# Attention scores by 64-row matmuls without the zero half of the keys, even and odd heads in two PSUM banks

## The chip, the cores and the metric

The kernel runs on one core of one Trainium2 chip. The metric is the device time of one launch in microseconds (us). A core has several engines that run side by side and meet at semaphores: TensorE (PE: matmuls, PEld: its weight loads), VectorE (DVE), ScalarE (ACT), GpSimd (POOL) and SyncE (SP, which starts DMA transfers). Matmuls write to PSUM, which is cut into eight banks; all else lives in SBUF, 128 partitions wide.

## The reference

One layer of a graph network: 128 graphs of 64 nodes, 512 channels, 8 heads of 64 channels.

```python
nx = _layernorm(x, ln1_g, ln1_b)
q = (nx @ Wq + bq).reshape(B, S, HEADS, HEAD_DIM)      # B = 128 graphs, S = 64 nodes
k = (nx @ Wk + bk).reshape(B, S, HEADS, HEAD_DIM)
v = (nx @ Wv + bv).reshape(B, S, HEADS, HEAD_DIM)
scores = jnp.einsum('bqhd,bkhd->bhqk', q, k) / np.sqrt(HEAD_DIM)
scores = jnp.where(adj_mask[:, None, :, :], scores, NEG)
attn = jax.nn.softmax(scores, axis=-1)
out = jnp.einsum('bhqk,bkhd->bqhd', attn, v).reshape(B, S, H)
x = x + (out @ Wo + bo)
nx = _layernorm(x, ln2_g, ln2_b)
return x + jax.nn.gelu(nx @ W1 + b1, approximate=False) @ W2 + b2
```

All is float32. Attention stays inside a graph: for each graph and head a 64 x 64 matrix of scores, over 64 channels.

## The kernel before

The 8192 nodes are cut into 16 groups (`NG`) of 512 nodes; a group has 4 tiles (`TILES`) of 128 nodes, and a tile holds two graphs. Phase one does layernorm, attention and its projection, group by group, and stores x1 to DRAM. Phase two loads x1 again and does the MLP, group by group.

Each large product is taken as three matmuls in the fast float32 form (`split3`, L154 to L156), from operands split into a high and a low part. The small products of the attention (scores, transposes of the probabilities, probabilities times v) are plain float32 matmuls.

Every engine has its own instruction stream, written out by hand, with semaphores between them. On TensorE the list `ORDER` sets the order inside a group's body:

- "U" n: one of 12 units of 12 matmuls that make q, k (transposed: channels on partitions) and v of the next group, into one of four PSUM banks `lin`.
- "S" t: `score`, the scores of tile t of this group.
- "P" t: `prob_transposes`; "O" t: `attend`, probabilities times v; "W" t: `project`.

So "S" 0 is followed by two units, "S" 1 by a unit, "P" 0 and a unit, "S" 2 directly by "O" 0, and "S" 3 by "W" 0. The last group has the order `LAST_ORDER`, in which fewer matmuls lie between the scores.

The scores before. The 128 partitions of `qT` and `kT` hold 64 channels of an even head (rows 0 to 63) and 64 of the odd head behind it (rows 64 to 127); m counts the four pairs of heads. A matmul that runs over all 128 rows would add the two heads. So `kT` is stored with a zero half: for each pair, tile and graph it has 128 columns, 64 in which only the rows of the even head are filled, 64 in which only those of the odd head are. POOL writes the zeros once for each of the two buffers (`zero_kT`, L461), ACT fills one half of the rows at a time (`take_k`, L538, two activations of 64 x 512 for each unit). `score` (L1042) then needs one matmul for each pair m and graph a: 128 rows of qT by 64 columns held in the array, 128 columns streamed. The output of graph a lands on partitions 64a to 64a+63, so the two graphs use the two column halves of the array.

`ps_scores` has two banks, one for the even tiles and one for the odd ones. The matmuls of a tile wait until DVE has read the scores of two tiles before (`wait(pe, masked, n - 1)`). DVE reads them in `mask_and_shift` (L762): it copies the scores where the adjacency is set into a buffer that POOL has filled with a large negative number.

At the start POOL's stream is: small constants, zeros for kT buffer 0, the first rstd, half of wq_lo and all of wk_lo (the low parts of the weights, L465), zeros for kT buffer 1, zeros for `probT` (L474), the second rstd. DVE's stream at that time splits the first normalised inputs into `nxT_hi` (L746) and `nxT_lo` (L748), four of each, one for each 128 channels; the first unit on TensorE waits for each of the four (`nx_split`).

Of the kernel before, what the change touches and what calls it, by code (L numbers as in the profile page):

```python
# [38 lines left out]
P = 128  # L39
# [119 lines left out]
def adj_layer(nc, x_dram, adj, ln1_g, ln1_b, ln2_g, ln2_b, wq, bq, wk, bk, wv, bv, wo, bo, w1, b1, w2, b2, out_dram):  # L159
# [7 lines left out]
    with ctx:  # L167
# [23 lines left out]
        with ExitStack() as phase:  # L191
            sb = placer(phase)
            wqkv_hi, wqkv_lo = ([sb(f"w{c}_{s}", [P, KC, HID], F32R) for c in "qkv"] for s in ("hi", "lo"))
            nxT_hi = sb("nxT_hi", [P, KC, GT], F32R)
            nxT_lo = sb("nxT_lo", [P, KC, GT], F32R)
            z1T = sb("z1T", [P, KC, GT])
            x = [sb(f"x{i}", [P, TILES, HID]) for i in range(2)]


            qT0 = sb("qT0", [P, KC, GT])  # L200
            kT0 = sb("kT0", [P, TILES, KC, 2, 2, NODES])
            v0 = sb("v0", [P, TILES, HID])
            early_end = nc.sbuf_base

            wo_hi, wo_lo = (sb(f"wo_{s}", [P, KC, HID], F32R) for s in ("hi", "lo"))
            xres = sb("xres", [P, 2, HID])
            bv_all = sb("bv_all", [P, HID])
            bo_all = sb("bo_all", [P, HID])
            qT = [qT0, sb("qT1", [P, KC, GT])]
            kT = [kT0, sb("kT1", [P, TILES, KC, 2, 2, NODES])]  # L210
            v = [v0, sb("v1", [P, TILES, HID])]
            softmax = sb("softmax", [P, 2, 2, HEADS, NODES])
            scores, expd = softmax[:, 0], softmax[:, 1]
            prob = sb("prob", [P, 2, HEADS, NODES])


            probT = sb("probT", [P, 2, KC, 2, 2, NODES])
            attT_hi = sb("attT_hi", [P, 2, HID], F32R)
            attT_lo = sb("attT_lo", [P, 2, HID], F32R)
            mask = sb("mask", [P, 2, TILES, NODES], U8)  # L220
            w_hi, w_lo = wqkv_hi + [wo_hi], wqkv_lo + [wo_lo]
# [21 lines left out]

        with ExitStack() as phase:
            lin = [phase.enter_context(nc.psum_tensor(f"lin{i}", [P, GT], F32)) for i in range(LIN)]
            ps_scores = phase.enter_context(nc.psum_tensor("ps_scores", [P, 2, HEADS, NODES], F32))
            ps_probT = phase.enter_context(nc.psum_tensor("ps_probT", [P, 2, KC, P], F32))
        with ExitStack() as phase:
            ps_out = [phase.enter_context(nc.psum_tensor(f"ps_out{i}", [P, HID], F32)) for i in range(TILES)]
# [13 lines left out]
        w_loaded, w_hi_done, w_lo_done = ([sem(f"w{c}_{s}") for c in "qkvo"] for s in ("loaded", "hi_done", "lo_done"))  # L263
        cols_loaded, rows_loaded, mlp_cols_loaded = sem("cols_loaded"), sem("rows_loaded"), sem("mlp_cols_loaded")
        filled, ident_done = sem("filled"), sem("ident_done")
        k_zeroed, probT_zeroed = sem("k_zeroed"), sem("probT_zeroed")
        stats_done, moments_done, var_done = sem("stats_done"), sem("moments_done"), sem("var_done")
        rstd_done, zn_done, t_done = sem("rstd_done"), sem("zn_done"), sem("t_done")
        z_transposed = sem("z_transposed")
# [3 lines left out]
        shifted, exp_done, sum_done, inv_done = sem("shifted"), sem("exp_done"), sem("sum_done"), sem("inv_done")  # L273
        prob_done, pt_done, probT_done = sem("prob_done"), sem("pt_done"), sem("probT_done")
        o_done, att_hi_done, att_split = sem("o_done"), sem("att_hi_done"), sem("att_split")
        mask_passed, fill_passed, stats_passed = sem("mask_passed"), sem("fill_passed"), sem("stats_passed")
        proj_done, xres_biased, x1_done = sem("proj_done"), sem("xres_biased"), sem("x1_done")

# [124 lines left out]
        def _(pool):  # L403
# [53 lines left out]
                for t in range(TILES):  # L457
                    bias_x1(g, par, t)

            def zero_kT(par):  # L460
                pool.memset(kT[par][:, :, :, :, :, :], 0.0).then_inc(k_zeroed, 1)  # L461

            def weight_lo(i, part):
                pool.wait_ge(w_hi_done[i], 1)
                pool.tensor_tensor(w_lo[i][:, part, :], raw_w[i][:, part], w_hi[i][:, part, :].bitcast(F32),  # L465
                                   ALU.subtract).then_inc(w_lo_done[i], 1)

            zero_kT(0)
            rstd_of(0)
            weight_lo(0, slice(KC // 2, KC))  # L470
            weight_lo(1, slice(0, KC))
            zero_kT(1)
            for par in range(2):
                pool.memset(probT[:, par], 0.0).then_inc(probT_zeroed, 1)  # L474
            rstd_of(1)
# [25 lines left out]
        def _(act):  # L501
# [31 lines left out]

            def take_k(g, par, m, bank):
                act.wait_ge(u_done, units_through(g, 3 * m + 1))
                for h in range(2):
                    rows = slice(h * HD, (h + 1) * HD)
                    act.activation(kT[par][rows, :, m, :, h, :],  # L538
                                   lin[bank][rows, :].rearrange("p (t a n) -> p t a n", a=2, n=NODES), ACT.Identity,
                                   bias=cols[rows, 3, m:m + 1]).then_inc(k_done, 1)  # L540

            def exponent(g, t):
                act.wait_ge(shifted, TILES * g + t + 1)
# [126 lines left out]
            for m in range(KC):  # L670
                take_q(0, 0, m, bank_of(-1, "U", 3 * m))
            weight_hi(3)
            act.wait_ge(k_zeroed, 1)
            for m in range(KC):
                take_k(0, 0, m, bank_of(-1, "U", 3 * m + 1))
            for k in range(KC):
# [2 lines left out]

            for i in range(4):  # L680
                act.wait_ge(w_lo_done[i], 2 if i == 0 else 1)
            act.wait_ge(k_zeroed, 2)
            body(0, 0)
            with act.Fori(1, NG - 4, 2) as g:
                body(g, 1)
# [11 lines left out]
        def _(dve):  # L697
# [57 lines left out]
            def mask_and_shift(g, par, t):  # L755
                n = TILES * g + t
                if t == 0:
                    dve.wait_ge(mask_loaded[par], 8 * (g - par) + 16)
                dve.wait_ge(neg_filled, n + 1)
                wait_apart(dve, s_done, n + 1, mask_passed)  # L760
                flags = mask[:, par, t, :].unsqueeze(1).broadcast_to((P, HEADS, NODES))
                dve.copy_predicated(scores[:, t % 2], flags, ps_scores[:, t % 2]).then_inc(masked, 1)  # L762
                dve.wait_ge(masked, n + 1)

                dve.tensor_reduce(row_max[:, :], scores[:, t % 2], AX.X, ALU.max).then_inc(max_done, 1)
                dve.wait_ge(max_done, n + 1)
                dve.tensor_tensor(scores[:, t % 2], scores[:, t % 2],
                                  row_max[:, :].unsqueeze(2).broadcast_to((P, HEADS, NODES)),
                                  ALU.subtract).then_inc(shifted, 1)
# [218 lines left out]
        def _(pe):  # L988
            def take_bank(g, kind, n):

                bank, last = ring_place(g, kind, n)
                if last is not None:
                    i, kind, n = last
                    which = {"U": (q_done, k_done, v_done)[n % 3], "L": v_done, "T": nx_done, "O": att_split,
                             "W": x1_done}[kind]
                    if kind == "L":
                        pe.wait_ge(v_done, KC * i + n // 3 + 1)
                    elif kind == "U":
                        per = 2 if n % 3 == 1 else 1
                        pe.wait_ge(which, per * (KC * (i + 1) + n // 3 + 1))  # L1000
                    elif kind == "T":
                        pe.wait_ge(which, KC * (i + 2) + n + 1)
                    else:
                        pe.wait_ge(which, TILES * i + n + 1)
# [27 lines left out]
            def score(g, par, t):  # L1032
# [2 lines left out]
                n = TILES * g + t  # L1035
                if t == 0:
                    pe.wait_ge(q_done, KC * (g + 1))
                    pe.wait_ge(k_done, 2 * KC * (g + 1))
                wait(pe, masked, n - 1)
                for m in range(KC):  # L1040
                    for a in range(2):
                        mm = pe.matmul(ps_scores[a * NODES:(a + 1) * NODES, t % 2, 2 * m:2 * m + 2, :],  # L1042
                                       qT[par][:, m, t * P + a * NODES:t * P + (a + 1) * NODES],
                                       kT[par][:, t, m, a, :, :], start=True, stop=True)
                mm.then_inc(s_done, 1)

            def prob_transposes(g, t):
# [149 lines left out]
```

## Time and profile before

| | us |
|---|---|
| median of three runs | 2328.38 |
| lowest and highest of them | 2325.96, 2328.45 |
| span of the profiled execution, first to last instruction | 2325.1 |
| phase one, up to about | 910 |
| one group of phase one in the loop | 54.94 |
| score matmuls, 64 tiles | 70.0 busy |

The profile gives the span of the execution that was profiled and no time of its own for it; the runs lie 0.9 to 3.4 us above that span, which is what surrounds the first and the last instruction. A busy share says how long an engine had work, and the chain of waits says what the end of the program hung on, step by step. Matmuls overlap: a float32 matmul record lasts much longer than the time until the next may start, so the chain's pieces, not the record's length, tell what a matmul costs. In the trace a plain float32 matmul shows up as two records, each with its weight load (1024 for the 512 of the scores).

### The profile page before, as it was taken

How to read it: one execution, taken by the hardware profiler on the slowest of the kernel's cores; microseconds unless marked ns; L12 is line 12 of the kernel's file. 1: busy time of each engine (PE TensorE's matmuls, PEld its weight loads, DVE VectorE, ACT ScalarE, POOL GpSimd, SP SyncE). 2: the span in 40 equal slices, each digit the busy share in tenths (PEclk: the TensorE clock that was granted, in tenths of full speed). 3: DMA queues.
4: the chain of work that ended last, by engine and by line, in shares of the span. 5: the costliest groups of instructions: out<-in, count | busy, mean ns of one | idle time of the engine just before them, and what ended most of it. 6: DMA issues, size and time to landing. Idle time of an engine off the chain costs nothing.

```text
span 2325.1 us, 30593 instructions
## 1 busy us (share of the span) xinstructions
PE 2288.6 (98%) x11568; PEld 1865.9 (80%) x11568; DVE 1200.6 (52%) x1975; ACT 792.8 (34%) x1298; POOL 291.7 (13%) x253
## 2 busy tenths in 40 slices
PE   6999999999999999999999999999999999999999
PEld 5787878788787877888888888888888888888887
DVE  5777777777777766434334334334334334334331
ACT  3444444444444444432222222222222222222222
POOL 3111111111111112620110110100100100100100
PEclk9999999999999999999999999999999999999999
DMA  4111121111111113311010010010010010010000
GB/s 137 51 56 56 60 70 66 55 55 55 55 55 60 41 47 104 127 37 37 1 37 26 11 37 23 15 37 21 16 37 20 18 37 19 19 37 19 19 19 19
DMA packets 67313, 99.29 MB, mean 43 GB/s; under 512 B 17680, under 2 KB 21776, under 8 KB 67216
## 3 DMA queue, kind: packets, MB, share of 16 engines
q1 hardware_dynamic: 61696, 97.27, 12.5%
q8 instruction: 83, 1.36, 0.3%
q10 hardware_dynamic: 5520, 0.55, 0.2%
q14 instruction: 14, 0.11, 0.0%
HBM read 64.25 MB, written 33.55 MB: 42 GB/s over the span
## 4 chain that ended last, share of the span: by engine, by line
PE 96%; DVE 2%; issue 1%; DMA 1%; ACT 0%; POOL 0%; SPq 0%; ACTq 0%; DVEq 0%
PE lin L154 11%; PE ps_out L154 10%; PE ps_out L156 10%; PE ps_out L155 10%; PE ps_h L155 10%; PE ps_h L154 10%; PE ps_h L156 10%; PE lin L155 10%; PE lin L156 10%; PE ps_scores L1042 3%; PE lin L1064 3%; PE ps_probT L1052 1%; DVE nxT_hi L746 1%; DMA raw<-in_L_gnn_W 0%; DMA x<-in_x 0%
## 5 line engine op out<-in xcount | busy, mean ns | idle before, releaser
L928 DVE TENSOR_TENSOR hT_lo<-hT,hT_hi 128x512 fp32r<-128x512 f32 x256 | 181.4, 709 | 856.8 <-ACT hT_hi L648 856.8
L638 ACT ACTIVATE hT<-ps_h,b_cols 128x512 f32<-128x512 f32 x256 | 176.6, 690 | 978.6 <-PE ps_h L156 978.6
L155 PE MATMUL ps_h<-mlp_nxT_lo,w_hi 128*128 128x512 f32 x1024 | 399.6, 390 | 4.9 <-issue 4.9
L154 PE MATMUL ps_h<-mlp_nxT_hi,w_lo 128*128 128x512 f32 x1024 | 399.1, 390 | 0.1
L154 PE MATMUL ps_out<-w_hi,hT_lo 128*128 128x512 f32 x1024 | 398.9, 390 | 0.3 <-POOL w_lo L453 0.3
L156 PE MATMUL ps_h<-mlp_nxT_hi,w_hi 128*128 128x512 f32 x1024 | 398.8, 389 | 0.0
L156 PE MATMUL ps_out<-w_hi,hT_hi 128*128 128x512 f32 x1024 | 398.8, 389 | 0.0
L155 PE MATMUL ps_out<-w_lo,hT_hi 128*128 128x512 f32 x1024 | 398.7, 389 | 0.0
L155 PEld LDWEIGHTS ps_h<-mlp_nxT_lo,w_hi 128*128 128x128 f32 x1024 | 192.2, 188 | 46.9 <-issue 7.4
L154 PEld LDWEIGHTS ps_h<-mlp_nxT_hi,w_lo 128*128 128x128 f32 x1024 | 192.1, 188 | 40.9 <-issue 1.0
L154 PEld LDWEIGHTS ps_out<-w_hi,hT_lo 128*128 128x128 f32 x1024 | 192.3, 188 | 40.4 <-issue 0.7
L156 PEld LDWEIGHTS ps_h<-mlp_nxT_hi,w_hi 128*128 128x128 f32 x1024 | 192.3, 188 | 40.0
L155 PEld LDWEIGHTS ps_out<-w_lo,hT_hi 128*128 128x128 f32 x1024 | 192.2, 188 | 39.9
L156 PEld LDWEIGHTS ps_out<-w_hi,hT_hi 128*128 128x128 f32 x1024 | 192.2, 188 | 39.8
L421 POOL TENSOR_TENSOR xres<-xres,bo_all 128x512 f32<-128x512 f32 x64 | 85.0, 1338 | 720.6 <-DMA xres<-in_x 720.6
L729 DVE STREAM_TRANSPOSE z2T<-zn 32x512 f32<-32x512 f32 x240 | 168.7, 703 | 4.9
L648 ACT ACTIVATE hT_hi<-hT 128x512 fp32r<-128x512 f32 x256 | 162.0, 633 | 13.6 <-DVE xres L796 3.3
L729 DVE STREAM_TRANSPOSE z1T<-x 32x512 f32<-32x512 f32 x224 | 157.3, 702 | 3.6
L442 POOL TENSOR_TENSOR rstd<-var_eps,minus_half 128x4 f32<-128x4 f32 x16 | 16.3, 1017 | 1007.8 <-DVE var_eps L894 1007.8
L154 PE MATMUL lin<-nxT_hi,wq_lo 128*128 128x512 f32 x256 | 106.2, 415 | 12.8 <-DVE nxT_lo L748 12.7
L538 ACT ACTIVATE kT<-lin,cols 64x512 f32<-64x512 f32 x128 | 87.6, 685 | 83.9 <-PE lin L156 82.3
L554 ACT ACTIVATE probT<-ps_probT 64x256 f32<-64x256 f32 x256 | 97.0, 379 | 49.3 <-PE ps_probT L1052 44.2
(90 smaller groups left out, 3223.8 us busy)
## 6 DMA issues: line engine op xcount, KB each, us to landing
xres<-in_x SPq DMA_DIRECT2D x64, 256.0 KB, 2.8
x_scratch<-xres SPq DMA_DIRECT2D x64, 256.0 KB, 2.0
x<-x_scratch SPq DMA_DIRECT2D x16, 1024.0 KB, 5.6
out<-x SPq DMA_DIRECT2D x64, 256.0 KB, 2.3
x<-in_x SPq DMA_DIRECT2D x15, 1024.0 KB, 5.9
raw<-in_L_gnn_W SPq DMA_DIRECT2D x16, 512.0 KB, 3.4
x<-in_x SPq DMA_DIRECT2D x4, 256.0 KB, 4.2
qT<-in_L_gnn_Wq SPq DMA_DIRECT2D x1, 1024.0 KB, 7.9
```

What stands on the lines that cost most here:

```text
L154: pe.matmul(out, lhs[1], rhs[0], start=first, stop=False)
L155: pe.matmul(out, lhs[0], rhs[1], start=False, stop=False)
L156: return pe.matmul(out, lhs[0], rhs[0], start=False, stop=last)
L421: pool.tensor_tensor(xres[:, t % 2], xres[:, t % 2], bo_all[:, :], ALU.add).then_inc(xres_biased, 1)
L538: act.activation(kT[par][rows, :, m, :, h, :], lin[bank][rows, :].rearrange("p (t a n) -> p t a n", a=2, n=NODES), ACT.Identity, bias=cols ...
L554: act.activation(probT[a * NODES:(a + 1) * NODES, t % 2, :, h, a, :], ps_probT[h * NODES:(h + 1) * NODES, t % 2, :, a * NODES:(a + 1) * NO ...
L638: act.activation(hT[:, m % 2], ps_h[m % 2][:, :], ACT.Gelu, bias=b1_cols[:, m:m + 1]).then_inc(gelu_done, 1)
L648: act.activation(hT_hi[:, m % HR], hT[:, m % 2], ACT.Copy).then_inc(h_hi_done, 1)
L729: return dve.transpose(to[channels, :, :].rearrange("p k (t n) -> p t k n", n=P)[:, :, :, tokens], source[tokens, :, :].rearrange("p t (k ...
L928: dve.tensor_tensor(hT_lo[:, m % HR], hT[:, m % 2], hT_hi[:, m % HR].bitcast(F32), ALU.subtract).then_inc(h_split, 1)
L1042: mm = pe.matmul(ps_scores[a * NODES:(a + 1) * NODES, t % 2, 2 * m:2 * m + 2, :], qT[par][:, m, t * P + a * NODES:t * P + (a + 1) * NODES] ...
L1064: mm = pe.matmul(bank[rows, (h // 2) * P:(h // 2 + 1) * P], v[par][:, t, h * HD:(h + 1) * HD], probT[:, t % 2, h // 2, h % 2, :, :], start ...
```

## The change

Scores are taken one head and graph at a time. A matmul uses only the 64 rows of its head (rows 0 to 63 or 64 to 127 of the array), 64 columns held and 64 streamed, so `kT` needs no zero half: it is stored like `qT`, with one activation of 128 x 512 for each unit. There are 16 matmuls for a tile in place of 8: first the four even heads for both graphs, then the four odd heads. Even heads go to one bank, odd heads to the other, and both banks hold the scores of even and odd tiles. A tile's matmuls therefore wait until DVE has read the tile just before. The DVE copy reads both banks by a strided pattern and writes the heads in their old places. `zero_kT` and its semaphore are gone, and a spare buffer of the same size keeps the layout of the memory.

```diff
-            kT0 = sb("kT0", [P, TILES, KC, 2, 2, NODES])
+            kT0 = sb("kT0", [P, KC, GT])
...
-            kT = [kT0, sb("kT1", [P, TILES, KC, 2, 2, NODES])]
+            kT = [kT0, sb("kT1", [P, KC, GT])]
...
-            ps_scores = phase.enter_context(nc.psum_tensor("ps_scores", [P, 2, HEADS, NODES], F32))
+            ps_scores = phase.enter_context(nc.psum_tensor("ps_scores", [P, 2, 2, KC, NODES], F32))
...
-            def zero_kT(par):
-                pool.memset(kT[par][:, :, :, :, :, :], 0.0).then_inc(k_zeroed, 1)
-
...
-            zero_kT(0)
             rstd_of(0)
             weight_lo(0, slice(KC // 2, KC))
             weight_lo(1, slice(0, KC))
-            zero_kT(1)
...
-                for h in range(2):
-                    rows = slice(h * HD, (h + 1) * HD)
-                    act.activation(kT[par][rows, :, m, :, h, :],
-                                   lin[bank][rows, :].rearrange("p (t a n) -> p t a n", a=2, n=NODES), ACT.Identity,
-                                   bias=cols[rows, 3, m:m + 1]).then_inc(k_done, 1)
+                act.activation(kT[par][:, m, :], lin[bank][:, :], ACT.Identity,
+                               bias=cols[:, 3, m:m + 1]).then_inc(k_done, 1)
...
-                flags = mask[:, par, t, :].unsqueeze(1).broadcast_to((P, HEADS, NODES))
-                dve.copy_predicated(scores[:, t % 2], flags, ps_scores[:, t % 2]).then_inc(masked, 1)
+                flags = mask[:, par, t, :].unsqueeze(1).unsqueeze(1).broadcast_to((P, 2, KC, NODES))
+                dve.copy_predicated(scores[:, t % 2].rearrange("p (m h) n -> p h m n", h=2), flags,
+                                    ps_scores[:, :, t % 2]).then_inc(masked, 1)
...
-                wait(pe, masked, n - 1)
-                for m in range(KC):
-                    for a in range(2):
-                        mm = pe.matmul(ps_scores[a * NODES:(a + 1) * NODES, t % 2, 2 * m:2 * m + 2, :],
-                                       qT[par][:, m, t * P + a * NODES:t * P + (a + 1) * NODES],
-                                       kT[par][:, t, m, a, :, :], start=True, stop=True)
+                wait_apart(pe, masked, n, score_passed)
+                for h in range(2):
+                    rows = slice(h * HD, (h + 1) * HD)
+                    for m in range(KC):
+                        for a in range(2):
+                            nodes = slice(t * P + a * NODES, t * P + (a + 1) * NODES)
+                            mm = pe.matmul(ps_scores[a * NODES:(a + 1) * NODES, h, t % 2, m, :],
+                                           qT[par][rows, m, nodes], kT[par][rows, m, nodes], start=True, stop=True)
```

TensorE's stream in the loop of phase one, at tile 2 of a group, before ("L156" ends a unit, `ps_scores` are the scores of tile 2, `lin<-probT,v` is "O" 0):

```order
L156 MATMUL lin<-nxT_hi,wq_hi 128x512
L1042 MATMUL ps_scores<-kT,qT 64x128 [waits masked]
L1042 MATMUL ps_scores<-kT,qT 64x128 x7
L1057 REGISTER_ALU [waits q_done]
L1064 MATMUL lin<-probT,v 64x128 [waits v_done,probT_done]
L1064 MATMUL lin<-probT,v 64x128 x7
```

The same place after the change:

```order
L156 MATMUL lin<-nxT_hi,wq_hi 128x512
L133 REGISTER_ALU
L1037 MATMUL ps_scores<-kT,qT 64x64 [waits masked]
L1037 MATMUL ps_scores<-kT,qT 64x64 x15
L1051 REGISTER_ALU [waits q_done]
L1058 MATMUL lin<-probT,v 64x128 [waits v_done,probT_done]
L1058 MATMUL lin<-probT,v 64x128 x7
```

Eight matmuls of 128 streamed columns have become sixteen of 64; "O" 0 still follows at once, and is now of another shape (128 rows against 64).

POOL's stream at the start, before and after in one piece (wq_lo and wk_lo are the low parts of the weights; the line numbers of the rows with + are those of the changed kernel):

```order
-L461 MEMSET kT 128x4096
-L412 TENSOR_TENSOR rstd<-var_eps,minus_half 128x4 [waits var_done]
-L465 TENSOR_TENSOR wq_lo<-qT,wq_hi 128x1024 [waits wq_hi_done]
-L465 TENSOR_TENSOR wk_lo<-v,wk_hi 128x2048 [waits wk_hi_done]
-L461 MEMSET kT 128x4096
-L474 MEMSET probT 128x1024 x2
+L414 TENSOR_TENSOR rstd<-var_eps,minus_half 128x4 [waits var_done]
+L464 TENSOR_TENSOR wq_lo<-qT,wq_hi 128x1024 [waits wq_hi_done]
+L464 TENSOR_TENSOR wk_lo<-v,wk_hi 128x2048 [waits wk_hi_done]
+L471 MEMSET probT 128x1024 x2
```

The two fills of kT are gone; the fills of probT follow wk_lo directly.

## Rows read from the trace of the kernel before

**Rows 1.** The page: busy time by engine; the chain that ended last.
```profile
PE 2288.6 (98%) x11568; PEld 1865.9 (80%) x11568; DVE 1200.6 (52%) x1975; ACT 792.8 (34%) x1298; POOL 291.7 (13%) x253
...
PE 96%; DVE 2%; issue 1%; DMA 1%; ACT 0%; POOL 0%; SPq 0%; ACTq 0%; DVEq 0%
```

**Rows 2.** Busy time in one loop group: stretch, engines, PEclk, DMA share, GB/s.
```profile
120.91:175.85 54.94, 54.94 (x337) 43.91 (x336) 40.76 (x70) 24.11 (x46) 8.54 (x9) 1.00 0.19 59
```

**Rows 3.** Groups of instructions, PE: busy us, mean ns, idle before.
```profile
L1042 PE MATMUL ps_scores<-kT,qT 128*64 128x128 f32 x1024 | 70.0, 279 | 0.0
L1064 PE MATMUL lin<-probT,v 128*64 128x128 f32 x1024 | 69.3, 278 | 0.3 <-issue 0.3
```

**Rows 4.** The chain of waits at tile 2: start us, us, what.
```profile
409.06 0.23 PE lin L155
409.29 0.23 PE lin L156
409.51 1.02 PE ps_scores L1042 x16
410.53 0.87 PE lin L1064 x16
411.41 0.43 PE lin L154
411.84 0.23 PE lin L155
```

**Rows 5.** Timeline, first records of tile 2's scores: start us, us, instruction.
```profile
354.51 0.33 PE L1042 MATMUL ps_scores<-kT,qT 128*64 128x128 f32 x2
354.50 0.14 PEld L1042 LDWEIGHTS ps_scores<-kT,qT 128*64 128x64 f32 x2 [0.35 <-issue]
...
354.56 0.14 PEld L1042 LDWEIGHTS ps_scores<-kT,qT 128*64 128x64 f32 x2
...
354.67 0.39 PE L1042 MATMUL ps_scores<-kT,qT 128*64 128x128 f32 x4
```

**Rows 6.** Timeline, start of the program, POOL.
```profile
1.47 3.51 POOL L461 MEMSET kT<- 128x4096 f32 x1
...
8.98 1.03 POOL L412 TENSOR_TENSOR rstd<-var_eps,minus_half 128x4 f32<-128x4 f32 x1 [4.00 <-DVE var_eps L717]
...
12.53 3.38 POOL L465 TENSOR_TENSOR wq_lo<-qT,wq_hi 128x1024 fp32r<-128x1024 f32 x1 [2.52 <-ACT wq_hi L509]
18.50 4.93 POOL L465 TENSOR_TENSOR wk_lo<-v,wk_hi 128x2048 fp32r<-128x2048 f32 x1 [2.60 <-ACT wk_hi L509]
23.38 3.50 POOL L461 MEMSET kT<- 128x4096 f32 x1
26.83 1.84 POOL L474 MEMSET probT<- 128x1024 f32 x2
```

**Rows 7.** Timeline, start of the program, DVE and PE.
```profile
14.65 1.54 DVE L746 CAST nxT_hi<-z1T 128x512 fp32r<-128x512 f32 x1 [0.95 <-ACT z1T L520]
16.83 0.42 DVE L746 CAST nxT_hi<-z1T 128x512 fp32r<-128x512 f32 x1
18.96 9.99 DVE L746 CAST nxT_hi<-z1T 128x512 fp32r<-128x512 f32 x1
28.98 0.69 DVE L748 TENSOR_TENSOR nxT_lo<-z1T,nxT_hi 128x512 fp32r<-128x512 f32 x1
29.73 0.80 PE L154 MATMUL lin<-nxT_hi,wq_lo 128*128 128x512 f32 x1 [9.03 <-DVE nxT_lo L748]
```

**Rows 8.** Stretches around that wait, as in rows 2.
```profile
23.31:29.72 6.41, 0.00 (x0) 0.00 (x0) 6.38 (x3) 0.00 (x0) 5.35 (x4) 0.50 0.54 127
29.72:33.60 3.88, 3.88 (x9) 3.10 (x10) 3.88 (x5) 0.69 (x1) 0.00 (x0) 0.50 0.00 0
```

**Rows 9.** Groups of instructions, ACT and DVE.
```profile
L538 ACT ACTIVATE kT<-lin,cols 64x512 f32<-64x512 f32 x128 | 87.6, 685 | 83.9 <-PE lin L156 82.3
L531 ACT ACTIVATE qT<-lin,cols 128x512 f32<-128x512 f32 x64 | 44.1, 689 | 121.4 <-PE lin L156 121.4
L762 DVE COPY_PREDICATED softmax<-mask,ps_scores 128x512 f32<-128x512 uint8 x64 | 46.8, 731 | 7.6 <-PE ps_scores L1042 5.8 <-POOL softmax L417 1.2
```

**Rows 10.** Timeline: DVE's read of one tile, PE's scores of the next.
```profile
398.19 0.73 DVE L762 COPY_PREDICATED softmax<-mask,ps_scores 128x512 f32<-128x512 uint8 x1
...
402.29 0.44 PE L1042 MATMUL ps_scores<-kT,qT 128*64 128x128 f32 x4
...
886.81 0.73 DVE L762 COPY_PREDICATED softmax<-mask,ps_scores 128x512 f32<-128x512 uint8 x1
...
887.92 1.09 PE L1042 MATMUL ps_scores<-kT,qT 128*64 128x128 f32 x16
```

More of the change, by code:

```diff
@@ L200, in adj_layer @@
             qT0 = sb("qT0", [P, KC, GT])
-            kT0 = sb("kT0", [P, TILES, KC, 2, 2, NODES])
+            kT0 = sb("kT0", [P, KC, GT])
             v0 = sb("v0", [P, TILES, HID])
+            sb("spare", [P, KC, GT])
             early_end = nc.sbuf_base
@@ L265, in adj_layer @@
         filled, ident_done = sem("filled"), sem("ident_done")
-        k_zeroed, probT_zeroed = sem("k_zeroed"), sem("probT_zeroed")
+        probT_zeroed = sem("probT_zeroed")
         stats_done, moments_done, var_done = sem("stats_done"), sem("moments_done"), sem("var_done")
@@ L275, in adj_layer @@
         o_done, att_hi_done, att_split = sem("o_done"), sem("att_hi_done"), sem("att_split")
+        score_passed = sem("score_passed")
         mask_passed, fill_passed, stats_passed = sem("mask_passed"), sem("fill_passed"), sem("stats_passed")
@@ L672, in _ @@
             weight_hi(3)
-            act.wait_ge(k_zeroed, 1)
             for m in range(KC):
@@ L681, in _ @@
                 act.wait_ge(w_lo_done[i], 2 if i == 0 else 1)
-            act.wait_ge(k_zeroed, 2)
             body(0, 0)
@@ L998, in take_bank @@
                     elif kind == "U":
-                        per = 2 if n % 3 == 1 else 1
-                        pe.wait_ge(which, per * (KC * (i + 1) + n // 3 + 1))
+                        pe.wait_ge(which, KC * (i + 1) + n // 3 + 1)
                     elif kind == "T":
@@ L1037, in score @@
                     pe.wait_ge(q_done, KC * (g + 1))
-                    pe.wait_ge(k_done, 2 * KC * (g + 1))
-                wait(pe, masked, n - 1)
-                for m in range(KC):
-                    for a in range(2):
-                        mm = pe.matmul(ps_scores[a * NODES:(a + 1) * NODES, t % 2, 2 * m:2 * m + 2, :],
-                                       qT[par][:, m, t * P + a * NODES:t * P + (a + 1) * NODES],
-                                       kT[par][:, t, m, a, :, :], start=True, stop=True)
+                    pe.wait_ge(k_done, KC * (g + 1))
+                wait_apart(pe, masked, n, score_passed)
[6 more added lines that the diff above has]
+                                           qT[par][rows, m, nodes], kT[par][rows, m, nodes], start=True, stop=True)
                 mm.then_inc(s_done, 1)
```

## The prediction

> **What bounds the kernel now.** I read the page first, then the chain of waits, then one group of phase one. TensorE is busy 98% of the span, and 96% of the chain that ended last is TensorE [rows 1]: nearly every microsecond taken from its stream or added to it shows in the time. In a group of the loop it is busy for all 54.94 us, with DVE at 40.76 and ACT at 24.11 [rows 2]. The grouped rows of the scores and of probabilities times v show no idle time worth counting before them [rows 3]. So the question is what the scores cost in the chain, and whether anything changes in the few places where TensorE waits. The longest such wait, 9.03 us, is at the start [rows 7].
>
> The length of a record (279 ns) is not its cost. In the chain the scores of a tile take 1.02 us for 16 records, and "O" 0, of the same shape and directly behind, takes 0.87 [rows 4]. 0.87 is the bare price of eight pairs of records, 0.109 us a pair; the scores pay 0.15 more because they follow a 128-column matmul. The matmul that comes after the pair takes 0.43 where its neighbours take 0.23 [rows 4], another 0.20 for the way back. The records come in twos: two loads at 354.50, two matmuls at 354.51, the next two loads at 354.56, the next two matmuls at 354.67 [rows 5]. I take the two of a pair to be the two graphs in the two column halves of the array, side by side.
>
> **The change part by part.**
>
> *Score matmuls.* 16 float32 matmuls in place of 8, so 32 records, 16 pairs. A pair's slot is set by what streams or by what loads. Streaming: 128 columns took 0.109, so 64 take 0.055. Loading: still 64 columns for each; the second pair of loads starts 0.06 after the first (354.50, 354.56 [rows 5]), while the first matmuls are in flight. Before, the loads were hidden under 0.109 of streaming; now both are of one size and must overlap fully. Lower end of a slot 0.055; upper end, nothing overlapped, 0.055 + 0.055 = 0.11. I take 0.057, near the two rows that bound it from below, since loads and matmuls overlap in these very rows. Of the 16 slots I count 15.5: when the stream passes from the even heads to the odd ones, it goes to other rows of the array, and their first load needn't wait. That is 15.5 x 0.057 = 0.88 against 0.87, +0.01 a tile, +0.6 us for 64 tiles (0.0095 unrounded). So the zero half goes and nothing is gained: half the columns, twice the matmuls.
>
> The row just used is also where the Trainium skill speaks against this change. "TensorE: Matmul & The Clock Gate", section "The mechanism" (Part 3), says that a weight load overlaps with matmuls in flight only when it goes to another row group. Here both pairs of loads are on all rows and the second still starts 0.05 us after the first matmul, so the trace disagrees. By that rule a slot would be a load plus a stream in every score; it is the rival "loads laid bare" below, and the sum by it would be 2384.
>
> *The way in and out.* 64-row matmuls are another shape of the array than 128 x 64. The way in exists before all 64 scores today and the way out behind 49 of them; there I keep 0.15 and 0.20. New is the way from "S" 2 to "O" 0, which today is free. It exists in groups 0 to 14; the last group has a unit between. The nearest row is the 0.15 that the scores pay after another shape: 15 x 0.15 = +2.3 us. Bounds: 0 if the chip makes no difference between 128 and 64 rows, and 0.20, the dearer of the two ways: 0 to +3.0. If the way into a 64-row shape cost 0.05 more or less than into a 128-row one, it would be 3.2 us more or less over 64 scores.
>
> *POOL's fills of kT.* The first is over at 4.98 us and POOL then idles until 8.98, so nothing waits for it [rows 6]. The second, 3.50 us, stands between wk_lo and the fills of probT [rows 6]. At the same time DVE's cast of nxT_hi takes 9.99 us where its neighbour takes 0.42, and ends at 28.95, 0.28 after POOL's last fill (28.67) [rows 6, 7]. An earlier cast shows the same: it starts under wq_lo and ends at 16.19, 0.28 after wq_lo (15.91). So the cast lies still until POOL is quiet; then nxT_lo (0.69) follows, and then TensorE, after 9.03 us of waiting. Without the fill POOL is quiet 3.50 us earlier: -3.5 us, and nothing else becomes late, for the same cast still ends last (at 25.45; wk_lo ends at 23.43). TensorE runs at half clock, granted 0.50, in this wait and for 3.88 us after it [rows 8]; I expect the same stretch at 1.2 GHz after an earlier restart, and no gain or loss from it. Bounds: -5.3 (the cast slips in behind wk_lo and is not held by the fills of probT) and 0 (the wait is set by something else).
>
> *ACT.* 64 activations of 128 x 512 (689 ns, as for qT) in place of 128 of 64 x 512 (685) [rows 9]: 43 us less, all of it beside TensorE, which never waits for ACT in the loop. Worth 0; TensorE is the cover.
>
> *DVE.* The copy has the same 128 x 512 elements, read from two banks in runs of 64. It takes 731 ns [rows 9]; even 0.1 more each would lie beside TensorE. Worth 0.
>
> *The new wait.* The scores of tile t now wait for DVE's read of tile t-1. The tightest place in the loop is tile 1: the read ends at 398.92, the scores start at 402.29 [rows 10], 3.4 us to spare. Behind the waiting instruction stand TensorE's scores and then the units, so a late read would stop everything, but it would have to be 3.4 us late. In the last group 0.38 us are left (887.54 to 887.92). Worth 0, with up to +1 in the last group.
>
> *Sum* against the profiled span: +0.6 + 2.3 - 3.5 = -0.6, 2325.1 to 2324.5. The span lies 3.3 us under the median of the runs, 2328.4; with the same around it the forecast is 2327.8, that is no change. What a measurement of this kernel can tell from no change is about 0.2%, 4.7 us (the three runs themselves spread over 2.5).
>
> **Rivals.**
>
> *Odd heads beside even heads.* If the odd heads' matmuls, on the other half of the rows and in the other bank, start while the even heads' are still running, four matmuls are in the array at a time. In full: 8 slots x 0.057 = 0.46 a tile, 0.41 less, x 64 = -26, with +2.3 - 3.5 -> 2301. In part (12 slots, 0.68): -12 -> 2315. For it: the pairs [rows 5] show that two parts of the array do work at once. Against: the order is all even heads, then all odd ones, 16 records apart, and the trace shows overlap only between records that stand near each other. Faster by 0.2% begins where a tile's scores fall to 0.82, 14.3 slots.
> The Trainium skill has the rule behind this rival: "TensorEngine Tiling (Array Packing)", section "Key Properties", says that tiles of the array work independently and in parallel, and that a change of mode drains it; of the first the trace shows column halves only, with the second the 0.15 and 0.20 of rows 4 agree.
>
> *Loads laid bare.* The mechanism that ends on the other side: in every score a pair's loads aren't hidden any more, because the stream over them is only as long as they are, or because TensorE cannot start 64 instructions in the time of 32. Slot 0.11, 16 x 0.11 = 1.76 a tile, +0.89 x 64 = +57, minus 1.2 -> 2384. It decides early: from a slot of 0.062 on (15.5 x 0.062 = 0.96) the kernel is 0.2% slower. For it: nothing in the trace has a stream this short over a load. Against: in the rows load and stream overlap, and two loads 0.06 apart leave room for one such slot.
>
> *The start gives nothing back.* The cast ends late for another reason than POOL: 2331. Against it: twice the same 0.28 behind POOL.
>
> **How the numbers follow.** The forecast's mechanism (slots of 0.055 to 0.065, new switches, shorter start) 0.66, with its own range 2321 to 2338: slots at 0.055 give 2326, at 0.065 give 2336 (15.5 x 0.008 x 64 = +8), switches +-3. Of that 0.42 lies within 0.2%, 0.10 below, 0.14 above. Odd beside even: 0.11 in part, 0.08 in full. Loads laid bare: 0.12. The rest, 0.03: the start or the wait goes wrong, mostly no change or slower. Faster 0.10 + 0.19, with a little of the rest, 0.30; same 0.42; slower 0.14 + 0.12 + 0.02, 0.28. The range 2308 to 2343 takes in the partial overlap and dear switches and leaves out 0.08 below and 0.12 above.
>
> **What would show it.** In the chain: scores at 1.03 a tile (0.88 + 0.15), "O" 0 at 1.02 in place of 0.87, the matmul behind at 0.43 still. In the timeline: pairs of matmuls 0.057 apart. At the start: the long cast near 6.5 us, TensorE's wait near 5.5, a granted clock of 0.50 for some 3.9 us after it. A group of the loop at 55.1 to 55.2 us. I am wrong if a score shows 0.5 to 0.8 in the chain (odd beside even), or 1.5 and more (loads laid bare), or if TensorE waits for a DVE read in the loop.

## The result, and the profile after

| kernel | median us | runs | span of the profiled execution |
|---|---|---|---|
| before (the forecast's three runs and one more) | 2327.17 | 2325.74 to 2328.45 | 2325.1 |
| after | 2340.11 | 2338.79 to 2340.68 | 2337.0 |

The ratio is 1.0054, 95% interval [1.0039, 1.0068]. The change costs 12.9 us by the medians, 11.9 by the spans. The forecast was 2327.8, no change.

The page of after: busy time, granted clock, instruction queue, chain.

```profile
PE 2295.1 (98%) x12592; PEld 1871.7 (80%) x12592; DVE 1191.5 (51%) x1975; ACT 746.2 (32%) x1234; POOL 287.9 (12%) x251
...
q8 instruction: 131, 2.15, 0.4%
...
PE 96%; DVE 2%; issue 1%; DMA 1%; ACT 0%; POOL 0%; SPq 0%; ACTq 0%; DVEq 0%
```

This looks like [rows 1], and none of it shows the cause at a glance. The waits of TensorE do (line waited for, us in total, times, longest):

```profile
PE lin L1149 <- DVE x L714: 11.0, 1, 11.0
PE ps_scores L1037 <- issue: 9.2, 5, 2.1
PE lin L154 <- DVE nxT_lo L740: 8.8, 5, 5.0
PE ps_h L155 <- issue: 4.3, 6, 1.1
```

The second line is new. "issue" means that TensorE waited for nothing that the profile shows. It happens five times, once in each pass of phase one's loop but the first, in the first scores behind the jump back. The timeline of PE at the first of them (start us, us, instruction, idle before):

```profile
226.33 0.39 PE L156 MATMUL lin<-wo_hi,attT_hi 128*128 128x512 f32 x1
226.65 0.68 PE L1037 MATMUL ps_scores<-kT,qT 64*64 64x64 f32 x19
229.26 0.62 PE L1037 MATMUL ps_scores<-kT,qT 64*64 64x64 f32 x13 [1.94 <-issue]
229.81 0.50 PE L154 MATMUL lin<-nxT_hi,wq_lo 128*128 128x512 f32 x1
```

19 of the 32 matmuls of one tile run, 1.94 us of nothing follows, then the other 13. Behind each of the five gaps lies a stretch in which the granted clock is at half, the 1.2 GHz level (stretch, its length, busy PE, PEld, DVE, ACT, POOL, PEclk, DMA share, GB/s):

```profile
231.20:234.50 3.30, 3.30 (x10) 2.58 (x9) 2.17 (x4) 0.15 (x1) 0.00 (x0) 0.51 0.85 285
343.90:347.10 3.20, 3.20 (x9) 2.52 (x8) 2.39 (x4) 0.00 (x0) 0.00 (x0) 0.51 0.77 221
456.50:459.70 3.20, 3.20 (x9) 2.46 (x9) 3.13 (x5) 0.00 (x0) 0.00 (x0) 0.50 0.78 225
569.10:572.40 3.30, 3.30 (x8) 2.60 (x9) 3.22 (x5) 0.00 (x0) 0.00 (x0) 0.51 0.59 170
681.80:688.40 6.60, 6.60 (x27) 5.22 (x28) 3.30 (x5) 0.24 (x1) 0.00 (x0) 0.50 0.85 263
```

19.6 us at half rate are 9.8 us lost. So the gaps cost 9.2 + 9.8 = 19.0 us by these rows, more than the whole difference; the rest of the change must have gained. The chain at tile 2 shows where, beside [rows 4]:

```profile
411.62 0.23 PE lin L156
411.84 0.91 PE ps_scores L1037 x30
412.75 1.02 PE lin L1058 x16
413.77 0.43 PE lin L154
```

The scores take 0.91 where they took 1.02, "O" 0 takes 1.02 where it took 0.87, and the matmul behind is at 0.43 as before. The start, beside [rows 6, 7] (POOL, DVE and PE):

```profile
18.75 4.92 POOL L464 TENSOR_TENSOR wk_lo<-v,wk_hi 128x2048 fp32r<-128x2048 f32 x1 [2.61 <-ACT wk_hi L506]
19.21 6.53 DVE L738 CAST nxT_hi<-z1T 128x512 fp32r<-128x512 f32 x1
23.63 1.83 POOL L471 MEMSET probT<- 128x1024 f32 x2
25.77 0.69 DVE L740 TENSOR_TENSOR nxT_lo<-z1T,nxT_hi 128x512 fp32r<-128x512 f32 x1
26.52 0.80 PE L154 MATMUL lin<-nxT_hi,wq_lo 128*128 128x512 f32 x1 [5.04 <-DVE nxT_lo L740]
```

The budget of the spans, in us: scores (0.91 - 1.02) x 64 = -7.0; the new switch 15 x 0.15 = +2.3; the start -3.6 (TensorE goes on at 26.52 in place of 29.73, and of the next 3.88 us 11 matmuls are seen where before there were 9 [rows 8], some 0.4); the gaps +9.2; half clock +9.8. The sum is +10.7, measured +11.9. The records of TensorE's sequencer show its jumps back and take up part of the 1.2 left over: the five passes from the loop's first jump back to its end take 567.1 us in after and 546.8 in e6 below, which is the same kernel without the gaps, so the gaps cost 20.3 us and not 19.0. The MLP's loop, which has gaps in both kernels, is 0.9 shorter in after. With both the sum is +11.1; 0.8 stay unassigned.

### The profile page after: what moved, and what is told of

It reads as the page before. It is cut to its first block, busy times and chain, and to the rows that moved or that the text cites. A ratio compares the mean times of both kernels' runs of the same rounds, so it can differ in the third digit from the quotient of the medians.

```text
span 2337.0 us, 32573 instructions
## 1 busy us (share of the span) xinstructions
PE 2295.1 (98%) x12592; PEld 1871.7 (80%) x12592; DVE 1191.5 (51%) x1975; ACT 746.2 (32%) x1234; POOL 287.9 (12%) x251
## 3 DMA queue, kind: packets, MB, share of 16 engines
q8 instruction: 131, 2.15, 0.4%
## 4 chain that ended last, share of the span: by engine, by line
PE 96%; DVE 2%; issue 1%; DMA 1%; ACT 0%; POOL 0%; SPq 0%; ACTq 0%; DVEq 0%
PE lin L154 11%; PE lin L156 10%; PE ps_out L156 10%; PE ps_out L154 10%; PE ps_out L155 10%; PE lin L155 10%; PE ps_h L155 10%; PE ps_h L156 10%; PE ps_h L154 10%; PE lin L1058 3%; PE ps_scores L1037 2%; PE ps_probT L1046 1%; DVE nxT_hi L738 0%; DMA raw<-in_L_gnn_W 0%; DMA x<-in_x 0%
## 5 line engine op out<-in xcount | busy, mean ns | idle before, releaser
L156 PE MATMUL ps_h<-mlp_nxT_hi,w_hi 128*128 128x512 f32 x1024 | 398.4, 389 | 0.0
L156 PE MATMUL ps_out<-w_hi,hT_hi 128*128 128x512 f32 x1024 | 398.3, 389 | 0.0
L156 PEld LDWEIGHTS ps_out<-w_hi,hT_hi 128*128 128x128 f32 x1024 | 192.2, 188 | 39.7
L156 PEld LDWEIGHTS ps_h<-mlp_nxT_hi,w_hi 128*128 128x128 f32 x1024 | 192.2, 188 | 39.5
L154 PE MATMUL lin<-nxT_hi,wk_lo 128*128 128x512 f32 x256 | 105.0, 410 | 0.0
```

The lines of the kernel that those rows point to most:

```text
L154: pe.matmul(out, lhs[1], rhs[0], start=first, stop=False)
L156: return pe.matmul(out, lhs[0], rhs[0], start=False, stop=last)
```

## The experiments

Each time is the median of five runs (six in e1, twelve in e3, e4 and e5, four in e9, eleven in e13), with runs of the kernel before beside it on the same chip; ratios are to these. The kernel before stood at 2326.44 (beside e1 to e5), 2325.36 (e6 to e9), 2327.16 (e10), 2328.56 (e11, e12) and 2328.16 (e13).

The question was where the gaps come from. The first clue: q8, the queue that brings instructions, has 131 packets against 83 in the kernel before, 48 more of 16.4 KB each (2.15 MB in 131). The page of before:

```profile
q8 instruction: 83, 1.36, 0.3%
```

**e1: the changed kernel, TensorE's phase-one loop written out**

```diff
-            with pe.Fori(1, NG - 4, 2) as g:
-                body(g, 1)
-                body(g + 1, 0)
-            for g in range(NG - 3, NG):
+            for g in range(1, NG):
```

> The changed kernel with TensorE's loop of phase one written out: groups 1 to 15 stand one behind the other in its stream, the other engines keep their loops. Theory 'loop body': TensorE's loop of two groups grew from 1399 to 1655 instructions and is now fetched anew on each pass; the five gaps of 1.5 to 2.1 us before ps_scores (9.2 us in the waits) and the six half-clock stretches behind them (20.5 us granted 0.50 between 231 and 688 us, worth half of that, 10.2) both go: 2340.1 - 19.4 = about 2321. Rival 'the array half used': the clock falls because 64-row matmuls keep the array less busy; then the stretches at 0.50 stay without a gap before them, and the time is about 2331. Rival 'new wait': the gaps come from the wait for DVE's read; then they stay, and the time is 2340.

Measured: 2315.37 us, 0.9954 [0.9941, 0.9967], q8 at 63 packets. Both "issue" lines are gone from the waits, the MLP's too, which the expectation had not reckoned with (the MLP's loop is as it was, but it lies elsewhere in the longer program):

```profile
PE lin L1149 <- DVE x L714: 10.9, 1, 10.9
PE lin L154 <- DVE nxT_lo L740: 9.3, 5, 5.5
PE ps_t L1103 <- DVE zn L896: 3.4, 1, 3.4
PE ps_out L154 <- POOL w_lo L455: 1.8, 1, 1.8
PE lin L1058 <- issue: 0.4, 1, 0.4
```

The same matmuls in the same order, without the jump back: no gap. So the gaps belong to the loop, not to the scores' work or their waits.

**e3: the kernel before, its loop padded to the length of the changed one** (256 semaphore increments that nobody waits for, two behind every third matmul of the units and of `project`)

```diff
+                    if not isinstance(g, int):
+                        for _ in range(PAD):
+                            pe.sem_inc(padded, 1)
```

> The kernel before, scores untouched, with 256 semaphore increments more in TensorE's loop body (two behind every three matmuls), so that the body has as many instructions as in the changed kernel, 1655. Theory 'loop body': gaps of 1 to 2 us in the first scores behind each branch and half-clock stretches behind them, 2327 + 10 to 19 = 2337 to 2346. Rival 'short instructions': the gap comes from 64 instructions in 0.9 us directly behind the branch, whatever the size of the body; then no gap here, 2327.

Measured: 2326.84, 1.0005 [0.9997, 1.0014], 84 packets, no gap in phase one. The theory that the length of the loop's program alone decides fell here. Counted in the built programs, both loops are 103.4 KB long; they begin at different places, the padded one 4.18 blocks of 16 KB behind the first instruction, the changed kernel's 4.68 behind it. All such positions here are counts in the programs; no trace shows them.

**e4: the kernel before, the second kT buffer filled later**

```diff
-            zero_kT(1)
...
+            zero_kT(1)
```

> The kernel before with POOL's second fill of kT moved behind its second rstd: the start's part of the change alone. The long cast on DVE should take 6.5 us in place of 9.99, TensorE's wait for it 5.0 to 5.5 in place of 9.0. If only the wait counts: 2327.2 - 3.5 = 2323.7. If the half-clock stretch at the start goes too, as it did in the changed kernel (3.88 us at 0.50 cost 1.9): 2321.8. Rival 'something else held the cast': 2327.

Measured: 2322.84, 0.9987 [0.9978, 0.9995]: 3.6 us less than before by the medians, 2.7 by the spans. TensorE's wait for nxT_lo falls from 9.0 to 5.5 us. The start's term holds by itself, but the stretch at half rate behind the wait grows: matmuls stand 0.43 us apart until 31.77, 5.7 us behind the restart, against 3.9 in the kernel before. That gives back some 0.9 us.

**e5: the changed kernel, a unit ahead of the first scores**

```diff
-ORDER = [("S", 0), ("U", 0), ("U", 1), ("S", 1), ("U", 2), ("P", 0), ("U", 3), ("S", 2), ("O", 0), ("U", 4),
+ORDER = [("U", 0), ("S", 0), ("U", 1), ("S", 1), ("U", 2), ("P", 0), ("U", 3), ("S", 2), ("O", 0), ("U", 4),
```

> The changed kernel with the first unit of a group ahead of the first scores, so that twelve 512-column matmuls stand behind the loop's branch and not 64 short instructions; the body keeps its size. Theory 'loop body': the instructions are still fetched anew, so a gap of 0.5 to 1.5 us stays behind each branch, now before a unit's matmul; what is left of gap and half clock costs 4 to 12 us over 2321: 2325 to 2333. Rival 'short instructions': no gap, 2321.

Measured: 2326.01, 1.0002 [0.9993, 1.001]. q8 still has 131 packets, so the loop is still fetched anew, but the gap at the scores is gone: long matmuls now stand behind the jump. Part of the gain goes to a new wait, since the unit needs nxT_lo earlier:

```profile
PE lin L154 <- DVE nxT_lo L740: 12.0, 19, 5.0
```

Fetching and stalling are thus two things. The next theory: the place of the loop in the program decides whether it is fetched anew, namely when it touches 8 blocks of 16 KB. The next four kernels move the loops with increments in group 0's units, which run once, ahead of the loop:

```diff
+SHIFT = 2
...
+                    for _ in range(SHIFT if is_first(g - 1) else 0):
+                        pe.sem_inc(padded, 1)
```

SHIFT = 2 is 96 increments (0.375 blocks).

**e6: the changed kernel, shifted by 96**

> The changed kernel with 96 semaphore increments put into TensorE's program ahead of the phase-one loop (in group 0's units), nothing else. The loop's program keeps its length (103.4 KB) but lies in 7 blocks of 16 KB, not 8, and so does the MLP loop. Theory 'block span' (a loop is fetched anew in each pass if it touches 8 blocks): instruction packets fall from 131 to at most 84, the issue gaps of 9.2 us before the first scores and the half clock behind them are gone, the MLP loop's 4.3 us of issue gaps too: 2314 to 2320 us. Rival 'size of the loop's program': 131 packets and 2340 us as before the shift. Rival 'short matmuls use up instructions faster than they are fetched': gaps stay, about 2335 us.

Measured: 2314.11, 0.9948 [0.9934, 0.9961]; 32 packets; no gap in either loop.

```profile
q8 instruction: 32, 0.52, 0.1%
```

This is the changed kernel with nothing but 96 idle increments, and by the ratios to the kernel before (1.0054 without them, 0.9948 with them) it is 1.1% faster, some 25 us.

**e7: the padded kernel before, shifted by 144** (SHIFT = 3, PAD = 2)

> The kernel before with its phase-one loop padded by semaphore increments to the changed kernel's 103.4 KB (that alone gave 2326.8 us and 84 packets), now with 144 more increments ahead of the loop, so that it touches 8 blocks of 16 KB in place of 7; the scores are the old ones, 32 matmuls of 128 columns. Theory 'block span': instruction packets rise by about 48, TensorE gets gaps of 1 to 2 us once a pass with a stretch of half clock behind most of them, and the MLP loop's gaps (3.8 us) go: 2332 to 2342 us. Rival 'short matmuls': no gap in phase one and 2323 to 2327 us, since the old scores keep TensorE busy for longer per instruction.

Measured: 2335.77, 1.0040 [1.0026, 1.0053], 75 packets. The old scores get the gap, in each of the five passes behind the 11th matmul record:

```profile
232.54 0.86 PE L1047 MATMUL ps_scores<-kT,qT 128*64 128x128 f32 x11
235.62 0.49 PE L1047 MATMUL ps_scores<-kT,qT 128*64 128x128 f32 x5 [2.22 <-issue]
```

So it isn't the 64-row matmul that makes the gaps; moving a padded loop of the kernel before by 9 KB does it too.

**e8: the kernel before with the late fill, shifted by 96** (e4's diff and the shift)

> The kernel before with the second key buffer filled later (that alone gave 2322.8 us) and 96 increments ahead of the loop; phase-one loop and MLP loop then lie in 7 blocks each. Theory 'block span': MLP gaps of about 4.3 us go, 2317 to 2320 us. It is then the base against which the shifted changed kernel shows what the 64-row scores are worth by themselves: by the chain 0.91 + 1.02 in place of 1.02 + 0.87, so +0.04 us a tile (+2.6 us), by the busy time of TensorE a gain of about 3 us. Rival: the MLP's gaps have another cause, 2322 to 2323 us.

Measured: 2316.04, 0.9956 [0.9942, 0.9969]; 29 packets, no gap in the MLP. Against e6 it says what the change is worth when neither kernel is fetched anew: the spans are 2315.8 and 2313.4, the intervals of the ratios overlap. A pass of the loop settles it. In the records of TensorE's sequencer there are 109.87 us from one jump back to the next in the kernel before (109.84 to 109.90 here), in every pass, and 109.36 in e6: -0.51 for 8 tiles. The chain's numbers give 8 x (-0.11) + 2 x 0.15 = -0.58. The MLP's loop takes 174.08 us a pass in e6 and in e8, and 175.0 to 175.9 in the kernel before: there its fetching anew costs 7.2 us over the six passes, more than the 4.9 of its "issue" waits.

**e9: e6 with the head as innermost index**

```diff
-                for h in range(2):
-                    rows = slice(h * HD, (h + 1) * HD)
-                    for m in range(KC):
-                        for a in range(2):
+                for m in range(KC):
+                    for a in range(2):
+                        for h in range(2):
+                            rows = slice(h * HD, (h + 1) * HD)
```

> The changed kernel with the head as the innermost index of the score loop (an even head's matmuls and the odd head's of the same graph next to each other, on different 64 rows of the array) and the 96 increments ahead of the loop. Theory 'odd heads run beside even heads where they are adjacent': the scores in the chain fall from 0.91 us to between 0.46 and 0.6 us a tile, up to 0.3 to 0.45 us x 64 tiles = 19 to 29 us below the shifted changed kernel, 2287 to 2300 us. Rival 'matmuls begin in program order, one slot of 0.058 us a pair': scores stay at 0.91 to 1.0 us, 2314 to 2320 us. Rival 'changing rows costs the array a drain each time': scores over 1.3 us, above 2340 us.

Measured: 2298.91, 0.9881 [0.9866, 0.9896], the fastest kernel of the study, 26 us under the kernel before beside it. The chain has the scores at 0.62, with the 0.15 for the switch in it:

```profile
398.25 0.23 PE lin L156
398.70 0.62 PE ps_scores L1041 x32
399.32 1.02 PE lin L1062 x16
400.35 0.43 PE lin L155
```

A pass takes 107.08, 2.28 under e6: 0.285 a tile, 0.29 by the chain. Odd heads run beside even ones where they are adjacent. The whole gain over e6 is 15.2 us, under the 19 to 29 expected: 64 tiles at 0.285 would be 18.2, and between 750 and 930 us TensorE waits for the probabilities and at "O" for 1.6 us more than in e6. The records also explain the 0.91 of the changed kernel. In its tile at 411.77 they start in twos, from the second pair on 0.058 us apart, but in the middle of the tile, where the even heads end and the odd ones begin, four start together three times (from 412.06, 412.17 and 412.23 on): three of the 16 slots are shared at this seam.

**e10: the changed kernel, shifted by 48** (SHIFT = 1)

> The changed kernel with 48 increments ahead of the phase-one loop, where 96 gave 2314.1 us. The loop's program then still begins just below a 16 KB boundary (at 4.86 blocks) and ends at 11.33, so it still touches 8 blocks. Theory 'block span': about 131 instruction packets (48 more than a loop in 7 blocks), the issue gaps of 1.5 to 2.1 us ahead of scores in each pass and half clock behind them: 2333 to 2342 us. Rival 'the increments themselves, or any shift of the program, take the gaps away': 2314 to 2328 us. The MLP loop lies at 22.93 to 29.12, 8 blocks, and should be fetched anew too, as in the changed kernel.

Measured: 2313.28, 0.9938 [0.9924, 0.9951], 32 packets. The expectation failed: no fetching anew, no gap. Blocks counted from the first instruction cannot be right. With f for the fraction of a block at which the phase-one loop (6.46 blocks) begins, it was fetched anew at 0.68 (after, e5) and 0.74 (e7), and not at 0.86, 0.05 and 0.18 (e10, e6, e3); the MLP loop (6.18 blocks) was at 0.75 and not at 0.93, 0.12, 0.31 and 0.43. One moved boundary, at 0.75 to 0.86 of a block, fits all of these. The gaps point to the same place: the changed kernel stops behind 19 matmul records, with their loads and a few others some 40 instructions, behind 4.68, which is 4.83.

**e11 and e12: the changed kernel, shifted by 144 and by 192** (SHIFT = 3 and 4)

> The changed kernel with 144 increments ahead of the phase-one loop. 48 and 96 increments had both taken the gaps away, 48 against the expectation: the boundaries of the fetched blocks cannot lie where instruction 0 of the program was taken to be. All ten kernels so far agree with blocks of 16 KB whose boundaries lie 0.75 to 0.86 of a block behind that place, a loop being fetched anew in every pass where it then touches 8 blocks. Theory 'block span, boundaries moved': the loop lies at 5.24 to 11.71, which touches 7 of the moved blocks; no gaps, 32 packets, 2312 to 2317 us. Rival 'any shift takes them away': the same.

> The changed kernel with 192 increments ahead of the loop, which then lies at 5.43 to 11.89. Theory 'block span, boundaries moved' (at 0.75 to 0.86): it touches 8 blocks again, the MLP loop (at 23.50) does not. So the gaps of about 9 us ahead of the scores and stretches of half clock behind them are back, with about 48 packets more (some 80), while the MLP loop's 4.3 us of gaps stay away: 2328 to 2338 us. Rival 'any shift takes the gaps away': 32 packets, 2312 to 2317 us. Rival 'boundaries at whole multiples from instruction 0' as first assumed: 7 blocks, also 2312 to 2317 us.

Measured: e11 2312.98, 0.9938 [0.9924, 0.9951], 32 packets; e12 2313.13, 0.9936 [0.9923, 0.9950], 77 packets:

```profile
q8 instruction: 77, 1.26, 0.2%
```

```profile
224.39 0.39 PE L157 MATMUL lin<-wo_hi,attT_hi 128*128 128x512 f32 x1
224.71 0.98 PE L1041 MATMUL ps_scores<-kT,qT 64*64 64x64 f32 x32
225.61 0.50 PE L155 MATMUL lin<-nxT_hi,wq_lo 128*128 128x512 f32 x1
```

The fetching came back as the moved boundary says (32 to 77), the gap did not, and a pass takes 109.36 as in e6. Half of the expectation held. So fetching anew is needed for a gap but isn't enough. What is: in the records of TensorE's sequencer the first operation behind the jump comes 3.4 to 3.8 us after it where the loop is fetched anew (after, e7, e12), 0.3 where it isn't (before, e11). The long matmuls still in hand cover that. In the first pass of the changed kernel it is at 226.17, and the gap ends at 229.26: the next block is there some 3.1 us after the first (2.9 to 3.2 in the five passes). What TensorE has to do between the loop's head and the boundary is the cover for that.

**e13: the changed kernel, shifted by 240** (SHIFT = 5)

> The changed kernel with 240 increments ahead of the phase-one loop, where 192 gave 2313.1 us: with 192 the loop was fetched anew (77 packets) but no gap came. Theory 'second block late': after the jump back the loop's first block has to be fetched, and the block behind it arrives about 3.0 us after the first (changed kernel: first operation after the branch at 226.30, TensorE's gap ends at 229.26); the gap is that time less TensorE's work between the loop's head and the block boundary. With 192 increments the boundary is some 102 instructions behind the head, with long matmuls before it (5 us of work): no gap. With 240 it is some 54 behind, inside the first scores (about 27 pairs, 0.85 us): gaps of about 2.1 us ahead of the last scores of each pass, 9 to 11 us in all, with stretches of half clock behind them, 2328 to 2342 us. The MLP loop is fetched anew again (packets 125 to 131 in all), but its boundary lies 18 long pairs behind the head (3.4 us), so it has no gap. Rival 'a shift of the program takes the gaps away': 2312 to 2317 us.

Measured: 2332.20 over eleven runs, 1.0019 [1.0010, 1.0028].

```profile
PE ps_scores L1041 <- issue: 9.8, 7, 2.1
```

```profile
228.47 0.85 PE L1041 MATMUL ps_scores<-kT,qT 64*64 64x64 f32 x27
231.23 0.38 PE L1041 MATMUL ps_scores<-kT,qT 64*64 64x64 f32 x5 [1.91 <-issue]
```

The gaps stand behind the 27th matmul record in all five passes, as computed, are 1.5 to 2.1 us long and with two short ones sum to 9.8. One part missed: 86 packets, not 125 to 131. The MLP loop, which ends by this count 0.04 of a block behind the boundary, was fetched anew in one of its six passes only (at 1709.2 us the next operation comes 3.5 us after the jump, in the others 0.3), which fits the 9 packets over e12. The count is good to about that.

The gap's place follows the boundary through three kernels: 11, 19 and 27 matmuls behind the head in e7, after and e13, each in all five passes.

## Why the prediction was wrong, point by point

**The sum left out a term of about +20 us.** That TensorE is busy for all of a group [rows 2] still holds in after, outside the gaps. The group itself was forecast at 55.1 to 55.2 us: a pass, which is two groups, takes 112.8 to 114.8 in after, and in e6, without gaps, 109.36, that is 54.68 a group. The step that failed: the prediction took the cost of 64 instructions in place of 32 only as a question of starting them in time ("because TensorE cannot start 64 instructions in the time of 32"), and put what they do to the length and the place of the loop's program at nothing, without a word on it. The change adds 256 instructions to the loop, 16 KB, and moves its head by 128. By that the loop came to touch 8 blocks, was fetched anew in each pass, and had short matmuls at its head. e6 (the same kernel, moved: 2314.11) and e7 (the kernel before, padded and moved: 2335.77) show it from both sides. The hint was in the trace of the kernel before: its MLP loop was already fetched anew and had gaps of its own.

```profile
PE ps_h L155 <- issue: 4.9, 6, 1.1
```

e4, which has its loops where the kernel before has them, shows 4.4 in this row; e8, the same kernel shifted, shows none, and its MLP loop takes 6.6 us less.

**The scores' term, +0.6, was mis-sized; measured -7.0.** The slot was right, 0.057 forecast, 0.058 in the records. The count of slots was not: 15.5 forecast; 0.91 less the 0.15 for the way in is 0.76, 13.1 slots, for the seam is three slots and not a half. "The trace shows overlap only between records that stand near each other" was the step that failed in this term, and "odd heads beside even heads" in part was the truth here (12 slots were priced at -12 us). In full it was priced at 0.46 a tile; e9 has 0.62 - 0.15 = 0.47.

**The switch from "S" 2 to "O" 0**, forecast 1.02 in place of 0.87: measured 1.02. Right, as was 0.43 behind it.

**The start**, forecast -3.5: the cast takes 6.53 ("near 6.5"), the wait 5.04 ("near 5.5"), and TensorE goes on 3.2 us earlier. e4 gives 3.6 by itself. The stretch at half rate behind the wait was forecast at 3.9 us. The clock's row says 1.00 there in after, but matmuls start 0.43 apart from 27.12 to 29.25, the spacing of half rate, so it was there and about 1 us shorter. In e4 and e6 it lasts 5.7 us. "The same stretch" was therefore a guess that missed by up to 1.8 us, worth half of that. In the profiled run of e12 the cast takes 4.76 us and ends 0.3 behind wk_lo, before the fills of probT are over, and TensorE goes on at 24.61: the bound of -5.3 was real; the same streams of POOL and DVE gave the late end in e6 and the early one in e12. The prediction's reading of [rows 7] has a slip without effect: the longest wait of TensorE is the one before its first instruction, 10.7 us, and not the 9.03.

**ACT, DVE, the new wait**, worth 0: the copy takes 736 ns against 731, kT's activations 44.1 us in place of 87.6 [rows 9], and no wait of TensorE for the copy appears in any list.

**"Loads laid bare"** fell: a slot is 0.058. The measured time lies inside the range for a reason that no rival had, so that is no merit. Without the fetching the terms would have given 2325.1 - 7.0 + 2.3 - 3.6 = 2316.8 for the span; e6, which has the MLP's 7.2 us back as well (2309.6), has 2313.4. Of the 3.8 missing, the longer half rate at the start is 1.0, and another 1.9 lies between the two loops, where e6 takes 404.0 us and after 402.1; so the terms hold to about 4 us and not better.

The trace agrees with the Trainium skill's page "TensorEngine Tiling (Array Packing)", section "Key Properties", that tiles of the array work independently: e9's 0.62 against 0.91.

What stays open: why one moved boundary lies at 0.83 of a block from the program's first instruction, whether 7 blocks is the size of what TensorE's sequencer keeps or the sign of something else, why the same gaps bring a stretch of half clock every time in one kernel and twice in five in another, and 0.8 us of the budget. Whether gaps behave so on more than one core was not tried.

## What to carry to other kernels

When a change adds or removes instructions in a loop, count the loop's program and look at q8 and at the "issue" waits before and after: moving the loop by 3 KB was worth more than 1% here (e10), more than the change itself, and a comparison of two variants without levelling this may compare their placement. Put long instructions at a loop's head (e5 against after: 0.5%), or move the head (e6: 1.1%). And where two matmuls use different rows and columns of the array, put them next to each other: that was worth 15 us here, while the order with eight of one kind and then eight of the other got only the seam.

## What the hardware showed that was not expected

- Instructions are fetched in packets of 16.4 KB. A loop of 5.46 blocks was not fetched anew in any kernel; of 6.46 and 6.18 it was at some places and not at others. Fetching anew takes 3.4 to 4.0 us at the jump and, by where the gaps of after, e7 and e13 end, another 2.9 to 3.4 to the next block; in e12 nothing of either shows in the time of a pass.
- A gap of 1.5 to 2.1 us in TensorE's work was followed, 0 to 1.9 us after its end, by 3.2 to 6.6 us at a granted clock of 0.50, in all five passes of after. In e13 and e7, with gaps as long, only two of the five had such a stretch behind them. The profiled run of e13, the fastest of its eleven, is 11.1 us shorter than that of after: 6.0 of it lie in the five passes, and 6.3 in the MLP's loop, which is not held up there.
- Matmuls on different rows and columns overlap four at a time: 32 of 64 x 64 float32 took 0.47 us, 0.76 where only the seam overlaps.
